# Waiting for one half of a PSUM tile instead of the newest eviction, in the projection stage of a transformer layer

## The reference

```python
x = x + attn(layernorm(x))      # 16 heads of 64, causal softmax
x = x + ffn(layernorm(x))       # 4096 hidden, ternary weights, 8-bit activations

# in attn
q = jnp.einsum('bpm,hmd->bphd', x, Q_w) + Q_b
k = jnp.einsum('bpm,hmd->bphd', x, K_w) + K_b
v = jnp.einsum('bpm,hmd->bphd', x, V_w) + V_b
logits = jnp.einsum('bqhd,bkhd->bhqk', q, k) / math.sqrt(D_HEAD)
...
return jnp.einsum('bqhd,hdm->bqm', attn, O_w) + O_b
```

## Time and profile before

| | |
|---|---|
| median of 3 runs | 4675.55 us |
| lowest and highest run | 4674.78, 4683.35 us |
| the profiled execution | 4704.38 us |
| its span, on the slowest core (core 1) | 4702.8 us |
| spans of the eight cores | 4653.0 to 4702.8 us |
| mean granted clock of TensorE, by core | 0.756 to 0.761 |

### The profile page before, as it was taken

The page is one execution under the profiler, slowest core; times in us unless marked ns, Lnnn a source line. Parts: engine busy times, 40 slices in busy tenths (PEclk is TensorE's granted clock), DMA queues, the critical chain, the costliest instruction groups (busy, mean ns, idle before and its releaser), DMA issues. The chain is left out here.

```text
span 4702.8 us, 49343 instructions; the slowest of 8 cores (4653.0 to 4702.8 us)
## 1 busy us (share of the span) xinstructions
PE 2817.5 (60%) x17576; PEld 1444.6 (31%) x17576; DVE 1715.4 (36%) x3961; ACT 1033.8 (22%) x1127; POOL 45.5 (1%) x68
## 2 busy tenths in 40 slices
PE   0066547778722217777785466567778546778665
PEld 0022213343311115444442122123334234444332
DVE  1121134332233355646544212132221446454643
ACT  0001113465511131101010011025447331111010
POOL 0000000000000000000000000000000000000000
PEclk9989856656555559889898698756665668989889
DMA  7510012211164303445454300000000013445444
GB/s 127 165 32 18 18 54 88 74 56 54 37 161 140 119 9 72 136 120 155 124 151 139 125 18 18 18 14 14 19 19 1 10 41 81 133 128 148 126 126 152
DMA packets 472110, 380.91 MB, mean 81 GB/s; under 512 B 340674, under 2 KB 373570, under 8 KB 466756
## 3 DMA queue, kind: packets, MB, share of 16 engines
q1 hardware_dynamic: 460612, 335.81, 25.2%
q0 software_dynamic: 11264, 41.95, 2.8%
HBM read 335.77 MB, written 41.94 MB: 80 GB/s over the span
## 5 line engine op out<-in xcount | busy, mean ns | idle before, releaser
L80 ACT ACTIVATE b_pt<-b_lp,b_cb 128x1024 bf16<-128x1024 f32 (+3 forms) x640 | 622.6, 986 | 556.2 <-PE b_lp L80 355.0
L80 PE MATMUL c_op<-c_w2b,c_hq 128*128 128x512 bf16 x2048 | 520.2, 400 | 255.9 <-DMA c_w2b<-w2t_s 193.9
L80 PE MATMUL c_hp<-c_xq,c_w1b 128*128 128x257 bf16 x4096 | 522.2, 282 | 66.9 <-ACT c_H L80 58.3
L80 PE MATMUL b_av<-V,b_pt 128*128 128x65 bf16 x5120 | 378.1, 238 | 206.2 <-ACT b_pt L80 145.3
L80 PEld LDWEIGHTS c_hp<-c_xq,c_w1b 128*128 128x128 bf16 x4096 | 409.5, 101 | 204.0 <-issue 104.8
L80 ACT ACTIVATE c_H<-c_hp,c_cb 128x512 bf16<-128x512 f32 x256 | 175.9, 687 | 1249.9 <-DVE c_H L80 575.0
L80 PEld LDWEIGHTS b_av<-V,b_pt 128*128 128x128 bf16 x5120 | 297.6, 125 | 421.1 <-issue 421.0
L80 PE MATMUL b_lp<-Q,K 64*128 64x512 bf16 x1280 | 371.4, 592 | 11.0 <-DVE x L80 9.3
L80 PEld LDWEIGHTS c_op<-c_w2b,c_hq 128*128 128x128 bf16 x2048 | 198.4, 101 | 554.2 <-issue 361.8
L80 DVE TENSOR_TENSOR c_H<-c_hp,c_g1b 128x514 bf16<-128x514 f32 x256 | 177.1, 692 | 470.0 <-PE c_hp L80 468.3
L80 DVE MEMSET b_pt<- 128x256 bf16 (+2 forms) x192 | 93.1, 485 | 623.1 <-PE b_lp L80 573.7
(11 more groups left out here) (124 smaller groups left out, 2323.2 us busy)
## 6 DMA issues: line engine op xcount, KB each, us to landing
c_w2b<-w2t_s SPq DMA_DIRECT2D x256, 512.0 KB, 5.3
c_w1b<-w1t_s SPq DMA_DIRECT2D x128, 512.0 KB, 4.3
pw_stg<-w SPq DMA_DIRECT2D x32, 1024.0 KB, 4.8
wq_st<-w SPq DMA_DIRECT2D x16, 2048.0 KB, 9.2
a_xt<-x SPq DMA_DIRECT2D x32, 512.0 KB, 3.6
b_xr<-x SPq DMA_DIRECT2D x32, 512.0 KB, 3.6
out<-c_obf POOLq DMA_DIRECT2D x32, 512.0 KB, 2.9
wq_s<-p_wbf POOLq DMA_DIRECT2D x16, 512.0 KB, 7.9
```

Source lines behind the costliest of these rows:

```text
L80: h = getattr(eng, en["name"])(*en["args"], **en["kwargs"])
```

## The change

In the V part the transpose tile gets twice its size and is used in two halves by turns, and the wait before the transposes of tile u is for the copy of tile u-2, no longer for that of u-1. In the Q/K part the counter values of the activations are kept apart for the two halves of `a_qk`, and a group waits for the newest activation that read the same half, which is that of two groups before. The instructions that compute are the same ones, in the same order on each engine.

```diff
-        tpp = es_a.enter_context(nc.psum_tensor(f"a_tp{s}", [128, 1024], BF16))
+        tpp = es_a.enter_context(nc.psum_tensor(f"a_tp{s}", [128, 2048], BF16))
...
-            sc_qk = 0
-            first_qk = True
+            sc_qk2 = [0, 0]
...
                     r.wait(r.tensor, ve, ve_ap[u])
-                    if u >= 1:
-                        r.wait(r.tensor, ve, ve_xh[u - 1])
+                    if u >= 2:
+                        r.wait(r.tensor, ve, ve_xh[u - 2])
+                    tb = (u % 2) * 1024
                     for c in range(8):
                         tn.inc(r.tensor.transpose(
-                            tpp[:, c * 128:(c + 1) * 128],
+                            tpp[:, tb + c * 128:tb + (c + 1) * 128],
                             xh[:, c * 128:(c + 1) * 128], ident_bf[:, :]))
                     tn_xh[u] = tn.v
                     r.wait(r.vector, tn, tn_xh[u])
                     ve_xh[u] = ve.inc(r.vector.tensor_copy(
                         xhat.rearrange("p (c t) -> p c t", c=8)
                         [:, :, u * 128:(u + 1) * 128],
-                        tpp.rearrange("p (c t) -> p c t", c=8)))
+                        tpp[:, tb:tb + 1024].rearrange("p (c t) -> p c t",
+                                                       c=8)))
                     r.wait(r.tensor, ve, ve_xh[u])
...
                     for oc in range(8):
                         off = (oc % 2) * 512
-                        if first_qk and W is QWb and oc < 2 and p == 0:
-                            pass
-                        else:
-                            r.wait(r.tensor, sc, sc_qk)
+                        if sc_qk2[oc % 2]:
+                            r.wait(r.tensor, sc, sc_qk2[oc % 2])
                         for mc in range(8):
...
                         r.wait(r.scalar, tn)
-                        sc_qk = sc.inc(r.scalar.activation(
+                        sc_qk2[oc % 2] = sc.inc(r.scalar.activation(
                             dstb[:, oc * S + p * 512:oc * S + (p + 1) * 512],
                             qkps[:, off:off + 512], AF.Identity,
                             bias=bias[:, oc:oc + 1]))
-                first_qk = False
```

## The result

| | before | changed |
|---|---|---|
| median, 10 runs each | 4683.58 us | 4585.33 us |
| lowest to highest | 4673.99 to 4705.04 | 4565.45 to 4614.35 |
| the profiled execution | 4704.38 | 4584.6 |
| spans of its cores | 4653.0 to 4702.8 | 4525.0 to 4583.1 |

The account below looks back on a forecast made before the run. The prediction took TensorE and ScalarE working in turn to set stage A's Q/K time. It summed 118 x 1.081 = 127.6 us, plus 0.0 for the transpose tile, off the 4675.55 median: 4548.0 us, range 4537 to 4574.

Parts of the forecast that it names:

- The step of a group, 2.815 to 1.734 us, 118 times: Stage A, Q/K part: waiting for the eviction two groups back shortens each step by 1.081 us, 127.6 us in all.
- The drain counts too: Stage A, Q/K part: 0.16 us a step of pipeline drain, counted as busy, is saved too; 127.6, not 110.0 us.
- case C: Rival: only TensorE's idle time in the Q/K parts comes back, 110.0 us, time 4565.6; chance 0.06.
- Nothing else becomes late: Stage A: nothing replaces the removed wait; VectorE's x statistics keep more than 20 us of cover under the Q/K part.
- The transpose half costs and gives nothing: V part of stage A: the doubled transpose tile costed at 0.0 us, its removed wait being already over each time.
- V parts move by 1 us or so: Stage A: clock switches shift each of eight V parts by 1 us either way, some 3 us; all one way 8.
- So I take the same 127.6 off the median.: Whole kernel: the gain reckoned from the profile is subtracted from the runs' median, 4675.55, giving 4548.0 us.
- Case A: Rival: dense Q/K matmuls lower TensorE's clock in part; at a quarter of the time, 54 us lost, 4602; chance 0.07.

Follow-up runs that it names:

- e9: Kernel before, with the w1 load put behind the first w2 load in each group of stage C; 4545.0 us, ratio 0.9637.
- e10: Changed kernel, with the w1 load put behind the first w2 load in each group of stage C, run again; 4417.1 us, ratio 0.9377.
- e3: Kernel before, with 14 of 16 loads left out of each pass over w2 (FFN output not the reference's); 4490.3 us.
- e4: Changed kernel, with 14 of 16 loads left out of each pass over w2 (FFN output not the reference's); 4364.2 us.
- e1: Kernel before with only the Q/K waits changed, transpose tile as before; 4584.8 us, ratio 0.9734.
- e5: The whole change measured again beside the kernel before, on one chip with its Q/K half alone; 4586.4 us, ratio 0.9715.
- e12: The whole change measured a third time beside the kernel before, to see chip-to-chip movement; 4589.3 us, ratio 0.973.
- e2: Kernel before with only the transpose tile doubled and its wait moved to tile u-2; 4708.7 us, ratio 1.0005.
- e8: Changed kernel, with the w1 load put behind the first w2 load in each group of stage C; 4418.6 us, ratio 0.9368.
- e7: Changed kernel, with each w2 load halved and TensorE starting once the first half has landed; 4463.6 us, ratio 0.9462.

## Why the prediction was wrong, point by point

- **The step of a group, 2.815 to 1.734 us, 118 times.** Right. The evictions are 1.73 us apart, the waits are gone, and e9 less e10 gives 127.9 us, e3 less e4 126.1, e1, e5 and e12 127.2, 128.2 and 127.0. Both stages A together take 676 to 678 us in the mean of the cores in the four profiles with the old waits (before, e2, e3, e9), and 544 to 548 in nine of the ten with the new ones; the tenth, e8, has 554, with the clock of the last section.
- **The drain counts too.** Right: on the profiled cores the matmuls of the eight Q/K parts took 351 to 352 us before and 222 after, 129 us less and not the 110.0 of case C. The medians alone could not tell the two apart, since the uncertainty of each difference is some 20 us or more; the cores' mean in e9 less e10, at least 124 us, could.
- **Nothing else becomes late.** Right. The statistics still run under the Q/K part, VectorE's idle time before a_st fell from 37.30 to 22.07 us.
- **The transpose half costs and gives nothing.** Right: e2, 1.0005. The waits for a_xm stayed.
- **V parts move by 1 us or so.** Right: between the Q/K parts of the profiled cores lie 39 to 44 us, before and after.
- **"So I take the same 127.6 off the median."** This is the step that failed. It carried a gain of each core over to the median of three runs of the slowest core, 4675.55, and gave it a range made of V parts and 1 to 2 us of the runs' spread. That spread was mis-sized: the ten runs before cover 31 us, the ten after 49, and the profile's 28.8 us above the median, which the prediction names, got no place in the range. The base was 8 us low: ten runs had 4683.6, from which the sum gives 4556.0, inside the range but still 29 us below the measurement. (The profiled execution, 4704.4, gives 4576.8, 8 us from what was measured; this is luck, since it was among the longest.) And the metric is the highest of eight cores, in which stage C's w2 waits count: in the profile of the kernel before, the second stage C took 925 us on one core and 950 on another, with 88 and 104 us of w2 waits, so a scatter of 25 us was there to be read.
- **Case A, a lowered clock.** It exists: e8's profile caught it (below). In the profile of the changed kernel all Q/K parts of all cores ran at 1.00. In the first comparison the slowest core has a mean clock of only 0.738 to 0.742 in four of the eleven executions of the changed kernel whose cores are on record; e8's four affected cores have 0.738 to 0.740. The other seven still have a median of 4584.6 us, with the slowest core 34 us above the mean, so this clock isn't the main thing that kept the median up. It does come more often with the change: some core lies 0.01 or more below its kernel's median clock in 12 of 65 executions with the new Q/K waits and in 3 of 62 with the old ones. These executions have no trace, so that it was the level of 0.81 in each is not shown.

Shown: the gain per core, that it reaches the slowest core in full in each later comparison, with w2's loads as they are (e1, e5, e12), taken out or issued in time, and that the transpose half has no part.

Not settled: why the first comparison gave 98 us. What the record shows narrows it. There, the mean over the cores is 4549.9 us with the change (median of eleven executions) and 4674.4 in the only execution of the kernel before whose cores are known, the profiled one: 124.5 us apart. On the other chips both means are 12 to 23 us higher, and so is stage C: both stages C together take 1901 us before and 1903 after in the mean of the cores of the first two profiles, 1915 in e2's and 1918 in e1's. So the first chip was quicker with both kernels, and the mean fell there about as forecast. The missing 30 us lie in what the slowest core adds to the mean: 40 us with the change, where e1, e5 and e12 have 23, 24 and 18; and by an estimate, 4683.6 less 4674.4, some 9 us before it, where the other chips have 14 to 19. Why the slowest core stood out so far on that chip stays open.

## What to carry to other kernels

A wait for the newest reader of a two-slot tile serialises producer and consumer although both slots exist; the timeline shows it as an idle time before every group, and its price is the change of the group's pitch, not the idle time, since the pipeline's drain comes back as well. When the metric is the slowest of several cores, give the range the scatter of every stage that waits for DMA, read core by core, and not only that of the stage which is changed; and compare twins, both with the disturbing stage calmed, if the size of a gain is in question. Before a slot is made larger for a late load, look in the queue at what stands ahead of it: here one swap of two lines was worth 168 us, more than the change under study. The length of the load counted too (e7).

## What the runs showed of the hardware that was not expected

The clock has a level between the two of the earlier trace rows. In e8's profiled execution cores 2 and 3 took 302 and 303 us for their first stage A, the other six 271 to 276. A window of core 2 in that stage (the last numbers being granted clock, DMA share and GB/s):

```profile
269.00:293.00 24.00, 20.84 (x80) 8.41 (x78) 1.11 (x6) 7.61 (x12) 0.00 (x0) 0.81 0.00 1
```

Two evictions of K in it begin at 285.74 and 287.84. They are 2.10 us apart, not 1.73: a matmul takes 0.263 us where it took 0.217. By this a Q/K part at 0.81 costs 16 x 0.37 = 6 us, four of them 24; the stage took some 28 us more than on the other cores, and the slower V parts would account for the rest. The page TensorE: Matmul & The Clock Gate of the Trainium skill describes such a level in its section Seeing it yourself, a peak-current limit at 13/16 of the clock that takes a whole die once three of its cores run dense matmuls. The level agrees with the 0.81 here. That the whole die is taken doesn't: cores 0 and 1 of the same die ran their first stage A in 276 us. In e8, cores 0 and 1 had the level later, in the second stage C, for about 250 us each, and cores 2 and 3 did not. In all three profiles with the level (e2, e8, e9) it came to two neighbouring cores at nearly the same time. Nor does it need the dense Q/K parts: e9, which has the old waits, ran at 0.81 for 146 and 152 us of stage C on cores 2 and 3, and e2, which has them too, shows it in its attention stage (core 6):

```profile
883.00:907.40 24.40, 19.97 (x82) 8.51 (x81) 7.08 (x6) 0.00 (x0) 0.00 (x0) 0.81 0.20 64
```
